# Value products of four heads per call in the first attention, and a fixed row region per expert in the first mixture of experts

## Time and profile before

| | us |
|---|---|
| median of 3 runs | 2289.98 (2289.2 to 2295.62) |
| the profiled execution | 2287.08 |
| its span | 2285.3 |
| TensorE busy | 1807.9 (79%) |
| VectorE busy | 1140.6 (50%) |
| ScalarE busy | 759.1 (33%) |
| GpSimd busy | 502.2 (22%) |

### The profile page before, as it was taken

How to read it: one execution, slowest core, us unless ns; L and a number is a source line. 1 busy time by engine, 2 the same in 40 slices (tenths; PEclk the granted TensorE clock), 3 DMA queues, 4 the chain that set the end, 5 groups by cost and what they waited for, 6 DMA issues and landing times. The chain is left out here.

```text
span 2285.3 us, 32329 instructions
## 1 busy us (share of the span) xinstructions
PE 1807.9 (79%) x9490; PEld 1178.8 (52%) x9490; DVE 1140.6 (50%) x3699; ACT 759.1 (33%) x1873; POOL 502.2 (22%) x728
## 2 busy tenths in 40 slices
PE   0049999998897989777763999768888888882998
PEld 0024444444665667554541677535666555661676
DVE  5346767673326766744552222156665666641111
ACT  0004444453231245221210221137555566630211
POOL 0130100001101122301111111114434444531122
PEclk9999999998997999899885999859998999995999
DMA  8444544444200000160000101030000010002332
GB/s 179 133 79 89 106 81 87 72 72 121 84 18 0 1 1 1 39 257 12 12 13 24 33 30 33 26 106 9 16 17 19 24 25 19 19 19 59 129 135 70
DMA packets 72299, 129.65 MB, mean 57 GB/s; under 512 B 23030, under 2 KB 59573, under 8 KB 67442
## 3 DMA queue, kind: packets, MB, share of 16 engines
q1 hardware_dynamic: 52636, 107.80, 18.1%
q0 software_dynamic: 17632, 14.26, 2.5%
q10 hardware_dynamic: 1893, 5.99, 0.8%
HBM read 89.79 MB, written 39.52 MB: 57 GB/s over the span
## 5 line engine op out<-in xcount | busy, mean ns | idle before, releaser
L2304 POOL TENSOR_SCALAR l_P<-l_P,l_ri 111x111 f32<-111x111 f32 (+1 forms) x256 | 178.3, 714 | 159.3 <-DVE l_ri L2492 158.4
L653 ACT ACTIVATE PT<-psT 111x666 f32<-111x666 f32 x192 | 139.4, 726 | 156.4 <-PE psT L734 156.0
L2586 ACT ACTIVATE l_P<-l_S,l_nm 111x111 f32<-111x111 f32 (+2 forms) x384 | 179.3, 471 | 32.7 <-DVE l_nm L2485 32.5
L554 DVE TENSOR_REDUCE mx<-psS 111x2 f32<-111x666 f32 x192 | 159.6, 847 | 25.7 <-PE psS L719 25.7
L745 PE MATMUL psO<-PT,vS 111*32 111x333 f32 x768 | 147.0, 461 | 0.1
L2706 PE MATMUL l_psP<-ident,l_P 111*111 111x111 f32 x768 | 108.8, 281 | 32.2 <-DVE l_PT L2501 27.6
L2706 PEld LDWEIGHTS l_psP<-ident,l_P 111*111 111x111 f32 x768 | 95.4, 189 | 62.9 <-issue 33.1
L2042 DVE COPY t_hT<-t_psG 128x512 f32<-128x512 f32 x56 | 36.1, 686 | 175.0 <-PE t_psG L2085 175.0
L2485 DVE CUSTOM_DVE_ANT_0 l_S<-l_psA,l_am 111x111 f32<-111x111 f32 (+1 forms) x256 | 79.0, 331 | 76.9 <-PE l_psA L2692 70.1
L2074 PE MATMUL t_psH<-expert_w,t_xT 128*128 x224 | 103.4, 606 | 1.5 <-DVE t_xT L2035 1.2
L2097 PE MATMUL t_psY<-expert_w,t_hT 128*128 x448 | 101.4, 379 | 0.6 <-ACT t_yb L2007 0.6
(11 more groups left out here) (401 smaller groups left out, 3744.4 us busy)
## 6 DMA issues: line engine op xcount, KB each, us to landing
expert_w<-in_moe_dram SPq DMA_DIRECT2D x8, 2048.0 KB, 24.6
c_w<-in_moe_dram SPq DMA_DIRECT2D x16, 1024.0 KB, 7.2
qs<-halves_scratch SPq DMA_DIRECT2D x128, 83.5 KB, 3.2
ks<-halves_scratch SPq DMA_DIRECT2D x128, 83.5 KB, 4.1
halves_scratch<-high SPq DMA_DIRECT2D x32, 167.0 KB, 3.0
halves_scratch<-low SPq DMA_DIRECT2D x32, 167.0 KB, 3.6
c_xb<-xs_scratch SPq DMA_DIRECT2D x8, 667.3 KB
xs_scratch<-zeros SPq DMA_DIRECT2D x6, 777.0 KB
```

The source lines that it names most:

```text
L554: v.tensor_reduce(mx[J % 2][:, t, c:c + 65:64], psS[s % 2][0:TT, :, 0:T], AX.X, ALU.max, negate=True).then_inc(max_done, 1)
L653: s_.activation(PT[jp % 2][:, :, a, :], psT[0:TT, :, 0:T], ACT.Exp).then_inc(exp_done, 1)
L2304: r = g.tensor_scalar(Pt, Pt, ri[:, c % 2, 2 * t + half:2 * t + half + 1], None, ALU.mult)
L2586: s_.activation(P[c % 4][:, half, at(t):at(t + 1)], Sm[:, half, at(t):at(t + 1)], ACT.Exp, bias=nm[:, c % 2, i:i + 1], scale=-1.0, accum_o ...
```

## The change

1. **attention16**: the 24 steps of a batch are reordered so that for each tile of keys two pairs of heads follow each other (`parts`), and `values` is called every second step for four heads in the four groups of 32 columns. `PT` becomes three tiles of two pairs. TensorE's order in a step becomes piece, `scores_less_most`, scores, values.
2. **masked_attention**: each expert gets a region of 2688 rows in `xs_scratch`, so a slot is 2688 * expert + rank, with no blocks to hand out; after the last batch `tiles()` computes for each of the 28 tiles its expert and its first row. 1/(1 + exp(-m)) goes into the row as a 258th column. Rows and slots are double buffered. The eps is added on VectorE, GpSimd only computes the power. VectorE's and TensorE's order of `psV` pieces becomes rl, v0, v1, v2, rk; `norm(b + 2)` runs ahead of rk. The hardware loop is one round shorter. SyncE writes h of each batch to a DRAM copy.
3. **Fill**: `xs_scratch` has 21632 rows of 258 floats (22.3 MB; 3.7 MB before), both targets are written from 128 partitions, and the wait moves to the quantised stage.
4. **top1_experts**: SyncE reads a tile's first row from SBUF ahead of its load; four input buffers; a second indirect DMA per tile fetches the tokens' rows of h. VectorE computes h + prob * y out of `psY`, statistics and the normalised row; the scattered row is both, 512 floats. ScalarE's copy is gone.
5. **alibi_attention**: `take`, `norm` and `scale_taken` are gone; x is fetched normalised; all of h is loaded once by one DMA (111 partitions x 24 rows of 1 KB), and VectorE waits for it ahead of the first row minima.

```diff
@@ attention16
+    NQ = NS // 2
-        PT = [sb(f"PT{i}", [TT, 2, NT, T]) for i in range(2)]
+        PT = [sb(f"PT{i}", [TT, 2, 2, T]) for i in range(NT)]
+        def parts(s):
+            return 2 * (s // 6) + s % 2, s % 6 // 2
             def exp(b, s):
-                jp, a = s // NT, s % NT
+                jp, a = parts(s)
                 act.wait_ge(st_done, NS * b + s + 1)
-                if a == 0 and some(NPAIR * b + jp - 1):
-                    act.wait_ge(pv_done, NPAIR * b + jp - 1)
-                s_.activation(PT[jp % 2][:, :, a, :], psT[0:TT, :, 0:T], ACT.Exp).then_inc(exp_done, 1)
+                if some(NQ * b + s // 2 - 2):
+                    act.wait_ge(pv_done, NQ * b + s // 2 - 2)
+                s_.activation(PT[a][:, jp % 2, :, :], psT[0:TT, :, 0:T], ACT.Exp).then_inc(exp_done, 1)
-            def values(b, p, s):
...
+            def values(b, p, u):
+                J, a = u // NT, u % NT
+                pe.wait_ge(exp_done, NS * b + 2 * u + 2)
+                if a == 0 and some(4 * b + J):
+                    pe.wait_ge(o_out, 4 * b + J)
+                for c in range(2):
+                    for half in range(2):
+                        n = 2 * c + half
+                        r = mm(psO[32 * n:32 * n + 32, 0:T], vS[p][:, a, 4 * J + n, :], PT[a][:, c, half, :],
+                               start=a == 0, stop=a == NT - 1)
+                r.then_inc(pv_done, 1)
                 for s in range(NS):
-                    if s + AHEAD < NS or not last:
-                        scores(*of(b, p, s + AHEAD))
-                    if s >= 2:
-                        values(b, p, s - 2)
-                    elif not first:
-                        values(b - 1, 1 - p, NS + s - 2)
                     for args in pieces(b, p, s, first, last):
                         piece(*args)
                     scores_less_most(b, p, s, first, last)
+                    if s + AHEAD < NS or not last:
+                        scores(*of(b, p, s + AHEAD))
+                    if s % 2 == 0:
+                        if s >= 2:
+                            values(b, p, s // 2 - 1)
+                        elif not first:
+                            values(b - 1, 1 - p, NQ - 1)
@@ Fill.write
-            parts = 128 if f.shape[0] % 128 == 0 else TT
-            flat = f.rearrange("(p r) c -> p (r c)", p=parts)
+            flat = f.rearrange("(p r) c -> p (r c)", p=128)
@@ masked_attention, GpSimd and VectorE
             def scale(b):
-                pool.wait_ge(stats_done, b + 1)
+                pool.wait_ge(eps_done, b + 1)
                 pool.sem_inc(begun, 1)
-                batch_scale(nc, pool, sh, sc_tmp, b, "plain", scale_done)
+                eps_scale(nc, sh, b).then_inc(scale_done, 1)
             def route_place(b, p, n):
...
                 v.tensor_tensor(before[:, 0, :], before[:, 2, :], count[:, 2, :], ALU.add).then_inc(v_out, 1)
+                v.tensor_tensor(w[:, :, :], w[:, :, :], oh[:, :, :], ALU.mult)
+                dve.wait_ge(p_ready, b + 1)
+                v.tensor_scalar(pe_m[:, :], pe_m[:, :], 1.0, None, ALU.add)
+                dve.drain()
+                v.tensor_reduce(sl[:, :], w[:, :, :], AX.X, ALU.add)
+                v.reciprocal(row[p][:, :, D + 1], pe_m[:, :])
+                dve.drain()
+                v.tensor_copy(slot[p][:, :], sl[:, :]).then_inc(slot_ready, 1)
...
                 row_max(0)
-                if not last:
-                    dve.wait_ge(piece_done, base(b))
-                    norm(b + 1)
                 row_max(1)
...
+                piece("rl", 0)
                 piece("v", 0)
-                piece("rl", 0)
                 combine(2)
                 piece("v", 1)
+                piece("v", 2)
+                if later(b):
+                    dve.wait_ge(piece_done, number("x", 1, b, first, last)[1] + 1)
+                    norm(b + 2)
                 piece("rk", 0)
-                piece("v", 2)
@@ top1_experts, VectorE (rows, sums) and GpSimd (fetch, scale, send)
+            def sums(s):
+                dve.wait_ge(y_done, s + 1)
+                dve.wait_ge(hb_in[s % 4], 16 * (s // 4 + 1))
+                if s >= 2:
+                    dve.wait_ge(y_sent[s % 2], 16 * (s // 2))
+                new = yb[s % 2][:, 0:D]
+                v.scalar_tensor_tensor(new, psY[:, 0:D], xb[s % 4][:, D + 1:D + 2], hb[s % 4][:, :], ALU.mult, ALU.add
+                                       ).then_inc(y_out, 1)
+                dve.drain()
+                v.bn_stats(mom[:, :], new)
...
             for s in range(NS):
                 hidden_out(s)
                 if s + 2 < NS:
                     input_out(s + 2)
+                if s >= 2:
+                    rows(s - 2)
+                if s >= 1:
+                    sums(s - 1)
+            rows(NS - 2)
+            sums(NS - 1)
+            rows(NS - 1)
@@ alibi_attention, SyncE and VectorE
+            sync.dma_start(sh.h[:, :, :], routed.ys[:, 0:D].rearrange("(n p) c -> p n c", p=TT)).then_inc(h_in, 16)
             fetch(1, 2)
             stream.prefetch(sync)
...
-            take(1)
+            dve.wait_ge(h_in, 16)
...
-                    if c == 0 and not last:
-                        norm(b + 1)
...
-                    if c == 6 and later(b):
-                        take(b + 2)
```

More of the change, by code:

```diff
@@ L1186, in dequantise, with quantised @@
         pool.drain()
-def quantised(nc, sh, pre):
+def quantised(nc, sh, pre, fill):
     NS = 3 * B
@@ L1462, in masked_attention @@
         bq = sb("bq", [128, KT])
-        sc_tmp = sb("tmp", [TT, 3, NT])
-        row = sb("row", [TT, NT, ROW1])
+        row = [sb(f"row{i}", [TT, NT, ROW1]) for i in range(2)]
         rT = sb("rT", [128, KT, T])
@@ L1505, in batches, with later @@
             body(0, 0, True, False)
-            with eng.Fori(0, (B - 2) // 2) as i:
+            with eng.Fori(0, (B - 4) // 2) as i:
                 body(2 * i + 1, 1, False, False)
                 body(2 * i + 2, 0, False, False)
-            body(B - 1, 1, False, True)
+            for b in range(B - 3, B):
+                body(b, b % 2, False, b == B - 1)
+        def later(b):
+            return not isinstance(b, int) or b + 2 < B
         def base(b):
@@ L1543, in _, with send @@
             experts.load(sync, ins["moe1"], range(E))
-            sync.wait_ge(scattered, 16 * NT * B)
+            def send(b):
+                sync.wait_ge(stats_done, b + 1)
+                sync.dma_start(routed.h[bass.ds(b * T, T), :].rearrange("(t p) c -> p t c", p=TT),
+                               sh.h[:, bass.ds(NT * b, NT), :]).then_inc(h_sent, 16)
+            batches(sync, lambda b, p, first, last: send(b))
+            sync.wait_ge(h_sent, 16 * B)
+            for p in range(2):
+                sync.wait_ge(scattered[p], 8 * NT * B)
         @block.gpsimd
@@ L1690, in route_place @@
-                dve.drain()
-                v.tensor_tensor(past_all[:, :], past_all[:, :], past_now[:, :], ALU.add)
-                dve.drain()
+                v.tensor_copy(routed.tile_row[:, :], used[:, :])
+                v.tensor_copy(routed.tile_expert[:, :], expert[:, :])
             norm(0)
+            dve.wait_ge(piece_done, 2)
+            norm(1)
             for t in range(NT):
@@ L1830, in _, with piece @@
             mm = nc.tensor.matmul
-            def piece(kind, j, b, place):
+            def piece(kind, j, b, p, place):
                 bank, n = place
@@ L1904, in some_piece @@
                             pe.wait_ge(piece_out, number("rx", 1, b, first, last)[1] + 1)
-                        piece(kind, j, b - 1 if kind in ("rx", "rl", "rk") else b + 1, number(kind, j, b, first, last))
+                        piece(kind, j, b - 1 if kind in ("rx", "rl", "rk") else b + 1, 1 - p,
+                              number(kind, j, b, first, last))
                 pe.wait_ge(piece_out, base(b))
@@ L2339, in body @@
                         row_rest(b - 1)
-                    if c == 7 and later(b):
-                        scale_taken(b + 2)
                     if c == 7 and not first:
@@ L2964, in program @@
                 quant = Quantised(nc, most, ins)
-                fill = Fill(nc, most, [routed.xs, xs2[0:E * CAP, :]])
+                fill = Fill(nc, most, [xs2[0:FILL2, :], routed.xs])
                 recurrence(nc, sh, quant, fill)
-                scan_layer(nc, sh, quant, fill)
-                quantised(nc, sh, quant)
+                scan_layer(nc, sh, quant)
+                quantised(nc, sh, quant, fill)
             masked_attention(nc, sh, ins, experts, routed)
```

298 lines of the change are left out of this document (145 added, 153 removed).

## The result

The changed kernel takes 2336.04 us (median of 4 runs, 2326.53 to 2341.74) against 2292.38 for the kernel before (4 runs): ratio 1.0186, interval 1.0148 to 1.0224. It is slower by 44 us. The forecast was 2215, in a range up to 2262: the wrong sign.

The account below looks back on a forecast made before the run. TensorE was taken to bound attention16 and top1_experts, with a psT-exponential chain just beneath, and waits masked_attention. 2287.1 - 18 - 36 + 4 + 6 - 31 = 2212, with 2.9 to the median 2215 us; range 2188 to 2262.

Parts of the forecast that it names:

- step 1: attention16: four-head value calls at 0.72 us shorten batches from 45.4 us; 2.3 a batch taken, -18 us in all.
- A: attention16: the four groups run two by two, 1.38 us a call; whole kernel 2271 us; chance 0.10.
- B: attention16: four streams overlap less well, by the skill's speedup figure; at 20% more a pass 2228 us; chance 0.10.
- rival E: attention16, values: column groups of one call run one after the other, 2.3 us a call; 2355 us; chance 0.04.
- The floor of 1.38: attention16: the chain of psT write and exponential takes at least 1.38 us a step, whatever TensorE does meanwhile.
- Step 2: Fill: 27.8 MB written instead of 9.2, from 128 partitions, 66 us, not late at a barrier; 0, +3 at worst.
- Step 3: masked_attention: shorter chains around v2, norm and GpSimd's power save 4.1 us a batch; -36 us, bounds -15 and -45.
- Step 4: top1_experts: steady state unchanged, +1 at the start for a register read, +3 at the end; +4 us.
- Step 5: Start of alibi_attention: the first row minimum waits for the load of all of h; +6 us, -3 to +15.
- Step 6: Batches of alibi_attention: without take, scatters and scaling start sooner, 5.1 us for six batches; -31 us, bounds -15 and -42.
- Rival C: masked_attention and alibi_attention batches: new waits replace the freed ones, each term at its lower bound; 2252 us; chance 0.13.

Follow-up runs that it names:

- e4_order_alone: Kernel before, with only TensorE's order in an attention16 step changed to piece, psT, scores, values, still two heads a call: 2398.13 us, ratio 1.0449.
- e2_pieces_first: Changed kernel, but VectorE in attention16 empties the piece before it takes the row maximum; TensorE's order stays as changed: 2221.97 us, ratio 0.9682 (two runs).
- e7_late_h: Changed kernel with TensorE's old order, four-head call one pair of steps later, and alibi_attention's wait for h behind the first batch's chunk 1: 2196.91 us.
- e1_scores_first: Changed kernel, but TensorE in attention16 issues the scores first in a step again, ahead of piece and psT: 2242.94 us, ratio 0.9781.
- e8_spread_loads: Changed kernel with TensorE's old order, later four-head call, and 111-partition loads in alibi_attention and capacity_experts split 96 and 15: 2188.32 us, ratio 0.9554.

## Why the prediction was wrong, step by step

**The step that failed is 1, four heads per call.** Its working priced TensorE's steps (0.64 + 0.72 + piece, at least 1.38) and the chain through ScalarE, and took every piece as emptied in time; to VectorE it gave 0.5 us a batch for bursts. The front part of this document says that TensorE's order in a step becomes piece, `psT`, scores, values. That line was never costed. It moves the scores behind the piece, past an engine that takes them in the old order, and e4_order_alone shows that this line alone costs the 102 us. Of a moved step it has to be asked who takes its result on the other engines, and in which order; the prediction asked that of `norm` and the v pieces in masked_attention, and not here.

**What was right in step 1.** The call for four heads costs 0.69 to 0.70 (281.93 to 282.62), for 0.72 taken: four column groups run side by side. Rivals A, B and E fall with it, and with B the efficiency of the three-group row of the Trainium skill (TensorE: Matmul & The Clock Gate, Part 3), which as an estimate would have made 0.87. The floor of 1.38 stands in every table of intervals. With the order repaired on VectorE the stage gains 8.9 us (406.6), with the call behind the most piece 27.3 (388.2), for the 18 forecast. Of the 42.6 us a batch, the twelve intervals behind even steps were right (23.8 in e2_pieces_first for 23.7), and the twelve behind odd ones were priced too low (20.4 for 18.9): an odd step has nothing but `psT` and scores behind the most piece, so mT's 0.6 us shows ahead of "ot" and v0 even there, two q/k steps take 2.1 for 1.96, and the batch is 44.2. That wait for mT had no term.

**The clock** had no term at all. The price of a stand was taken as its own length, in every bound; against e2_pieces_first the changed kernel has 74 us of slower instructions beside 44 us of idle time.

**Step 2, Fill:** right. In e4_order_alone, with the Fill of before, recurrence and scan take 260.9 us, against 261.2 changed and 257.6 before, and e2_pieces_first, with the new Fill, takes 257.6: the 3.6 is the spread of that stage. In the busy time by stretch it moves 417 GB/s from 716 to 722 us, beside a TensorE that is busy for all 6.

**Step 3, masked_attention:** -41.1 for -36, inside its bounds. Two batches of the changed kernel begin 25.1 us apart, for 31.2 before and 27 forecast, and TensorE waits 1.3 to 1.6 there, not 4.45. GpSimd's power follows its scatters at once (a scatter ends and the power starts at 1291.0).

```profile
1212.81 3.58 PE L1903 MATMUL m_psS<-m_kT,m_qT 128*111 128x333 f32 x8 [1.33 <-issue]
...
1237.92 4.15 PE L1903 MATMUL m_psS<-m_kT,m_qT 128*111 128x333 f32 x8 [1.63 <-issue]
```

**Step 4, top1_experts:** +5.8 for +4. A tile still takes 7.98 us although VectorE is busy 91 us for 47. The end is longer than taken: from the last y to the next stage 10.6 us (1547.34 to 1557.97) against 6.1 (1471.06 to 1477.15), +4.5 for +3. The last scatter starts 3.4 us behind the sum, after statistics, power and row:

```profile
1550.74 1.03 POOL L2057 DMA_INDIRECT ys_scratch<-t_yb,t_to  x1 [1.26 <-DVE t_yb L2112]
```

**Step 5, start of alibi_attention:** the mechanism right, the size not. VectorE waits 6.5 us for h, but the first row minimum comes 1.7 us later after the stage's start than before (51.4 for 49.7), not 6: the load ran at 73 GB/s (1576 to 1605) for the 66 taken, and landed some 4 us earlier for it. And the wait does not set the time: e7_late_h takes it away and gains nothing that its runs can tell.

**Step 6, batches of alibi_attention:** seven periods of value products fell by 29.8 us, for 31. The chunk that lasted 10.8 with `take` lasts 7.2:

```profile
1847.27 1.35 PE L2766 MATMUL l_psO<-l_PT,l_vS 111*64 111x333 f32 x12
1854.44 1.35 PE L2766 MATMUL l_psO<-l_PT,l_vS 111*64 111x333 f32 x12
```

Rival C of the prediction had the right shape, a new wait in the place of a freed one, in the wrong stages; rival E had the right stage and the wrong mechanism. Neither asked whether two engines that share a PSUM tile and a score buffer still take them in the same order.

## What to carry to other kernels

Two engines that hand each other two things per step must take them in the same order: a reordering on one is only half an edit until the other engine's program has been read. Lay the slack beside the handover with the least cover (here the long call behind the most piece), and give a stand on a full TensorE two prices, its length alone (most of e4_order_alone's loss) and its length with a clock that follows it (most of what the changed kernel loses against e2_pieces_first). A freed wait on a load is worth nothing while the next load waits in the same queue; spreading the loads helped where moving the waits did not.

## What the runs showed of the hardware

- Four value products of 32 columns in the four column groups take 0.69 us, as long as two did.
- The stand of 2.1 us shown above was followed by a stretch at the 1.2 GHz level (0.50 for 9.5 us); the changed kernel's stage ran at 0.79. In e4_order_alone a batch with four stands of 1.3 to 1.4 us stayed at 1.00, and its stage ran at 0.92; in e2_pieces_first a batch with stands of 0.6 stayed at 1.00.
- Pairs of half-height matmuls (64 rows) start 0.15 us behind a pair of the same kind and 0.24 to 0.33 beside the value products: 0.19 us more for the same five groups in e1_scores_first than in e2_pieces_first.
- Cutting 15 of 111 partitions off into a transfer of their own raised the DMA share while the loads ran (0.82 for 0.56 in the same stretch): in e8_spread_loads the wait for the first expert's rows (667 KB) fell from 15.8 to 5.5 us.
